# A two-layer transformer block on one core: the reciprocals of the row sums are kept in PSUM, and the bank of the weighted sums is given back behind the product that reads them

## What is computed

```
qkv = x @ w_attn + b_attn;  q, k = rope(q), rope(k)
scores = einsum('bhtd,bhsd->bhts', q, k), causal
attn = softmax(scores) * E ** (-0.5)
o = einsum('bhts,bhsd->bhtd', attn, v)        # per head: 512 rows x 32
return o @ w_proj + b_proj
```

## Time and profile before

| | us |
|---|---|
| median of 3 runs | 1322.21 |
| time of the profiled execution | 1322.04 |
| its span | 1320.3 |
| PE busy | 1192.8 (90%) |
| DVE busy | 992.8 (75%) |
| ACT busy | 766.9 (58%) |
| POOL busy | 574.8 (44%) |
| one usual iteration | 147.6 |

### The profile page before, as it was taken

The page is one execution under the profiler, slowest core; times in us unless marked ns, Lnnn a source line. Parts: engine busy times, 40 slices in busy tenths (PEclk is TensorE's granted clock), DMA queues, the critical chain, the costliest instruction groups (busy, mean ns, idle before and its releaser), DMA issues.

```text
span 1320.3 us, 24729 instructions
## 1 busy us (share of the span) xinstructions
PE 1192.8 (90%) x9300; PEld 650.0 (49%) x9300; DVE 992.8 (75%) x2884; ACT 766.9 (58%) x1410; POOL 574.8 (44%) x634
## 2 busy tenths in 40 slices
PE   6577789999999999999999999999999999988796
PEld 4123444555545554555545554555545554554352
DVE  4666976978887787968887887968887887776532
ACT  5418654666466755666466755666465755575470
POOL 1520602871159312971259313961259213961252
PEclk9786879999999999999999999999999999989799
DMA  8420221002300222012300222012300230001000
GB/s 327 126 97 2 49 69 45 1 18 68 109 1 3 57 62 76 1 24 68 104 1 2 57 80 58 1 26 66 104 1 2 57 89 16 2 9 49 9 1 32
DMA packets 47614, 65.08 MB, mean 49 GB/s; under 512 B 8549, under 2 KB 33157, under 8 KB 46087
## 3 DMA queue, kind: packets, MB, share of 16 engines
q1 hardware_dynamic: 47494, 63.51, 16.3%
HBM read 29.63 MB, written 8.39 MB: 29 GB/s over the span
## 4 chain that ended last, share of the span: by engine, by line
PE 53%; DVE 31%; ACT 9%; issue 3%; POOL 2%; DMA 1%; POOLq 0%; SPq 0%; DVEq 0%; ACTq 0%
PE gen L468 19%; PE down L511 17%; DVE score L1076 9%; PE pv L565 4%; PE score L537 4%; DVE hT L969 4%; DVE probs L969 2%; PE score L543 2%; PE gen L528 1%; DVE mx L1076 1%; POOL rstd L1402 1%; DVE qkn L1168 1%; DVE bn L1105 1%; ACT probs L817 1%; ACT qkn L761 1%
## 5 line engine op out<-in xcount | busy, mean ns | idle before, releaser
L1402 POOL TENSOR_TENSOR rstd<-veps,mhalf 128x1 f32<-128x1 f32 (+1 forms) x104 | 67.0, 645 | 503.9 <-DVE veps L1153 363.8
L817 ACT ACTIVATE probs<-score 128x512 f16<-128x512 f32 (+1 forms) x384 | 201.7, 525 | 130.5 <-PE score L537 130.4
L969 DVE TENSOR_TENSOR probs<-score,probs 128x512 f16<-128x512 f32 (+1 forms) x384 | 212.9, 595 | 64.3 <-ACT score L819 64.2
L468 PE MATMUL gen<-x2T,t1T 128*128 128x512 f16 x1024 | 242.5, 382 | 4.0 <-ACT x2T L760 2.5
L511 PE MATMUL down<-t2T,hT 128*128 128x512 f16 x1024 | 233.0, 380 | 3.5 <-DVE xn L1138 3.5
L819 ACT ACTIVATE score<-score 128x512 f32<-128x512 f32 (+1 forms) x384 | 204.5, 532 | 0.0
L468 PE MATMUL gen<-xT,wa 128*128 128x512 f16 x768 | 180.8, 387 | 4.0 <-DVE mx L1076 4.0
L1076 DVE CUSTOM_DVE_ANT_0 score<-score,mask_rows 128x512 f32<-128x512 f32 (+1 forms) x344 | 157.8, 521 | 0.0
L969 DVE TENSOR_TENSOR hT<-gen,hT 128x512 f16<-128x512 f32 x160 | 108.6, 685 | 64.0 <-ACT gen L780 25.3
L511 PEld LDWEIGHTS down<-t2T,hT 128*128 128x128 f16 x1024 | 96.5, 98 | 110.4 <-DVE xn L1138 4.7
L468 PEld LDWEIGHTS gen<-x2T,t1T 128*128 128x128 f16 x1024 | 95.4, 98 | 109.3 <-ACT x2T L760 5.2
(11 more groups left out here) (128 smaller groups left out, 1799.2 us busy)
## 6 DMA issues: line engine op xcount, KB each, us to landing
qk<-qkn SPq DMA_DIRECT2D x384, 64.0 KB, 2.0
xo<-x SPq DMA_DIRECT2D x8, 1024.0 KB, 5.6
hT<-x SPq DMA_DIRECT2D x8, 1024.0 KB, 6.5
out<-xn SPq DMA_DIRECT2D x32, 256.0 KB, 2.2
hT<-w_fc SPq DMA_DIRECT2D x4, 1024.0 KB, 13.9
hT<-w_down SPq DMA_DIRECT2D x4, 1024.0 KB, 5.4
t2T<-w_qk SPq DMA_DIRECT2D x2, 1024.0 KB, 8.5
probs<-w_v SPq DMA_DIRECT2D x1, 1024.0 KB, 18.8
```

The source lines that it names most:

```text
L468: mm = nc.tensor.matmul(bank[:, :], a, b, start=(start and n == 0), stop=(stop and n == len(pairs) - 1))
L817: nc.scalar.activation(probs[:, h % 2, HI, 512 * i:512 * i + n], score[i][:, 0:n], ACT.Exp, scale=1.0 / S_UP)
L969: return V.tensor_tensor(out, whole, hi, ALU.subtract)
```

## The change

The array `r_sum` in SBUF goes away. The reciprocals are written to columns 272 to 275 of the bank `pv`, and the product reads them there; its other input `oA` stays in SBUF. So the bank can no longer be given back by the sum L1188: that one now counts `o_sums`, for which the product waits, and the product counts `pv_drained`. The semaphore `o_ready` goes away, and what waited for it (the first turn of `xo` on PE) waits for `pv_drained`. No instruction is added, taken away or moved on any engine; an operand, an output and the semaphores change.

```
-        r_sum = sb("r_sum", [PARTS, 2, TB], f32)
...
-        H_SUM, H_SQ = 264, 268
+        H_SUM, H_SQ, R_SUM = 264, 268, 272
...
                 def o_turn(tb):
                     if tb == 0:
-                        pe.wait_ge(o_ready, HEADS * (j + 1))
+                        pe.wait_ge(pv_drained, HEADS * (j + 1))
...
                     res = pv[:, 0:VW * TB].rearrange("p (b w) -> p b w", b=TB)
-                    V.reciprocal(r_sum[:, h % 2, :], res[:, :, HD]).then_inc(o_recip, 1)
+                    V.reciprocal(pv[:, R_SUM:R_SUM + TB], res[:, :, HD]).then_inc(o_recip, 1)
                     pairs = bass.AP(pv, 0, [[512, PARTS], [VW, TB], [1, HD], [HD + 1, 2]])
-                    V.tensor_reduce(oA[:, h % 2, :, :], pairs, AX.X, ALU.add).then_inc(pv_drained, 1)
+                    V.tensor_reduce(oA[:, h % 2, :, :], pairs, AX.X, ALU.add).then_inc(o_sums, 1)
                     if h == 0 and nxt:
                         dve.wait_ge(xn_ready, TB * (j + 2))
                     dve.wait_ge(o_recip, n + 1)
-                    dve.wait_ge(pv_drained, n + 1)
+                    dve.wait_ge(o_sums, n + 1)
                     V.tensor_tensor(xo[:, :, HD * h:HD * (h + 1)], oA[:, h % 2, :, :],
-                                    r_sum[:, h % 2, :].unsqueeze(2).to_broadcast([PARTS, TB, HD]), ALU.mult
-                                    ).then_inc(o_ready, 1)
+                                    pv[:, R_SUM:R_SUM + TB].unsqueeze(2).to_broadcast([PARTS, TB, HD]), ALU.mult
+                                    ).then_inc(pv_drained, 1)
```

More of the change, by code:

```diff
@@ L278, in build @@
             sem(n) for n in ("oT_hi", "y_full", "y_ready", "xn2_ready", "x2T_hi", "fin_ready"))
-        m_neg, m_hi, o_sums, o_recip, o_ready, x1_ready = (
-            sem(n) for n in ("m_neg", "m_hi", "o_sums", "o_recip", "o_ready", "x1_ready"))
+        m_neg, m_hi, o_sums, o_recip, x1_ready = (
+            sem(n) for n in ("m_neg", "m_hi", "o_sums", "o_recip", "x1_ready"))
         bn_done = [sem(f"bn_done{i}") for i in range(4)]
```

## The result

The kernel after took 1326.93 us in the median of eight runs (1325.31 to 1328.03), the kernel before 1322.68 us (eight runs, 1320.37 to 1323.41) on the same chip: ratio 1.0035, 95% interval 1.0025 to 1.0044. The change makes the kernel slower by 0.35%, for a forecast of 0.4%. The profiled span went from 1320.3 to 1326.2 us. These 5.9 us are more than the 4.3 us between the medians: single executions of one kernel differ by 3 us, and the profiled one of the kernel after (1327.97 us) is among its longest.

A forecast was written before the change was run, and what follows sets the result against it. PE was taken to bound the usual iterations' heads 0 to 6. Terms of 7.0 (usual iterations), +0.5 (iteration 7) and -1.7 (iteration 0) gave +5.8 on 1322.04: 1327.8 us, +0.4%; 8 in 10 from 1323 to 1331.5.

The forecast's parts named there:

- The bank comes back later: Usual iterations: PE's matmul may start 0.54 us after the sum's end, not 0.15; 1.16 us each, six times 7.0 us.
- The stalls that go: DVE's products: all 20.0 us of stalls end, but 13 of them, in usual iterations, are worth nothing.
- Rival 1: Returned stalls decide, DVE being on the path in usual iterations too: 1310 us in full; chance 0.07.
- Iteration 0: DVE is the chain from head 3 to 7, so unstalled products shorten this iteration: -1.7 us.
- I take 1.8, less 0.14 for a late `weigh(14)`: Iteration 0: gain taken between 1.3 and 2.2 us, less lateness at that hand-over: -1.7 us.
- Iteration 7: Heads without queries and keys: -0.5 us at `weigh(4)` from head 1's stall, later costs; net +0.7, taken as +0.5.
- the +0.3 over heads 6 to 8: Last iteration's heads: a stall of 0.91 us gives back 0.2, two hand-overs cost 0.5.
- Price of the operands: Product with one input in PSUM stays at 0.29 us, bounds 0.28 and 0.33; nothing taken for the reciprocal.
- Rival 3: PSUM operands cost more in product and sum, +2.3 to +4.3 us on top: 1330 to 1332 us; chance 0.14.
- Rival 2: Short hand-overs' lateness is hidden, only the squares and head 14 cost: +2.0 us, 1324.0 us; chance 0.16.
- Rival 4: PE's new idle moments lower its granted clock in usual heads: 24 us more, 1352 us; chance 0.03.
- about 35: PE's waits for `pv` released by the product, not the sum: from 13 to about 35 or more in number.

The follow-up runs named there:

- run 4: The changed form in all heads but 5 and 14, which keep the form of the kernel before: 1323.50 us, ratio 1.0007 to the kernel before.
- Run 7: Kernel before with the changed form only in heads 0, 4 and 7 to 13 of every iteration: 1322.83 us, ratio 1.0003.
- run 5: Kernel before with POOL's sums of squares cut to one column in all steps but the first: 1319.20 us, ratio 0.9978.
- run 2: Kernel before with the changed form in iterations 1 to 6 alone: 1328.41 us, ratio 1.0045.
- run 6: Kernel before with the changed form only in heads 4, 5, 7 of iteration 0 and 1, 6 of iteration 7: 1318.97 us, ratio 0.9981.
- run 3: Kernel before with the changed form in iterations 0 and 7 alone: 1320.44 us, ratio 0.9991.
- run 1: Kernel before, reciprocals still in SBUF, with the bank given back behind the product in all heads: 1341.92 us, ratio 1.0148.

## Why the prediction was right, and where it was not

**The bank comes back later: right, term by term.** Starts of the weight loads in iteration 2, after against before, gave +0.11, +0.02, +0.10, +0.39, +0.13 and +0.39 us for `weigh(2)`, (3), (4), the squares, `weigh(7)` and (15); the prediction had 0.12, 0.01, 0.12, 0.39, 0.13, 0.39. That is 1.14 for 1.16, and 6.8 for 7.0 in six iterations. The 0.54 us from the sum's end to the matmul came out to a hundredth at all 15 hand-overs for which PE is listed as waiting, and run 4 takes the two large terms away alone. Run 7 shows the other side, that more than 0.54 us of distance means no cost.

**The stalls that go: right in the usual iterations.** All of them went, and in heads 1 and 2 the waits for ACT took their place; run 5 shows it for heads 0 to 2 without any late hand-over: no gain within the heads. For head 6 the kernel after shows it: behind its product, which was stalled by 0.93 us, the starts only get later, by the 0.13 us of `weigh(7)`, and stay so up to `weigh(14)`. Rival 1 (the stalls returned decide) falls there.

**Iteration 0: right place, wrong size.** The term was -1.7 and came out as -0.9. DVE's rows of the kernel after, to be read with the earlier trace rows:

```profile
145.61 0.29 DVE L1192 TENSOR_TENSOR xo<-oA,pv 128x128 f32<-128x128 f32 x1
145.81 1.67 DVE L1046 TENSOR_SCALAR hT<-hT,theta 128x2048 f32<-128x2048 f32 x1
...
149.72 2.10 DVE L1046 TENSOR_SCALAR hT<-hT,theta 128x2048 f32<-128x2048 f32 x1
```

The thresholding behind head 4 fell from 2.18 to 1.67 us, not to 1.28, and that behind head 5 only from 2.18 to 2.10: they still overlap a POOL instruction. That part of the working, by which the thresholding gets ahead of POOL's next instruction, didn't hold. Even so the lead was 1.95 us at head 8. The failed step is "I take 1.8, less 0.14 for a late `weigh(14)`": it took the lead at head 7 or 8 for what remains at the end. From head 8 to 9 it fell to 1.40, and in head 15 from 1.46 to 0.86. The window of 162 to 166 us, before and then after, in two fences (columns as in the earlier trace rows):

```profile
162.00:166.00 4.00, 1.77 (x28) 1.21 (x28) 3.62 (x15) 0.96 (x4) 2.77 (x3) 1.00 0.00 0
```
```profile
162.00:166.00 4.00, 3.24 (x25) 2.21 (x26) 2.78 (x10) 2.17 (x5) 1.92 (x2) 0.50 0.01 2
```

The kernel before had PE at 2.4 GHz (granted 1.00) there, the kernel after at 1.2 GHz (0.50). In the 4 us ahead of it PE was busy for 2.85 us before and 2.17 us after, both at the full clock still. Over all heads of this iteration the clock is 0.80, where it was 0.83:

```profile
126.00:198.00 72.00, 59.75 (x543) 35.41 (x541) 57.18 (x160) 45.13 (x96) 20.93 (x16) 0.80 0.22 57
```

That the clock took the missing 0.8 us is the likeliest reading, not shown: no run moved the clock alone, and iteration 0 with the old form differs by 0.56 us between the kernel before and run 2. In head 15 the late bank has a part: run 6, which doesn't hold it there, fell by 0.29 and not by 0.60.

**Iteration 7: +0.5 forecast, +0.5 measured, by another way.** The gain at head 1 was larger: `weigh(4)` was 0.95 us earlier than before within the iteration, not 0.5. Then the 16 down products behind it ran at half clock in part. They are shown before and after, in two fences:

```profile
1171.88 3.62 PE L511 MATMUL down<-t2T,hT 128*128 128x512 f16 x16
```
```profile
1176.94 4.68 PE L510 MATMUL down<-t2T,hT 128*128 128x512 f16 x16
```

The sum agrees by luck, and the prediction had the clock of these heads at its old level throughout. The slow stretch isn't the change's own: in run 2, with the old form there, these down products took 3.84 us, in run 3, with the new form, 3.62, and yet the heads of iteration 7 took 0.3 us less than before in run 2 and 0.3 more in run 3. The +0.39 at the squares and at head 14 stand. Of the terms between them, the +0.3 over heads 6 to 8 came out as a gain of 0.9 (in run 3 as a cost of 0.5), and the +0.15 at head 11 as nothing.

**The total: agreement in part by luck.** The profiled kernels differ by 5.9 us for a forecast of 5.8. Iteration 0 gave 0.8 us less than was taken; 0.4 us came back ahead of the first head, where nothing was changed, 0.2 in the usual iterations and 0.1 behind the heads.

**Price of the operands: right.** The product takes 288 ns where undisturbed ones took 293, so an input in PSUM costs nothing here. The two bounds were 0.28 and 0.33. The estimate of 65 ns more that followed from the Trainium skill (VectorE: DVE Perf Modes, the section on the TRN2 errata) isn't borne out; these rows decide. The reciprocal costs 9 ns more, and the sum behind it starts 0.09 us after its start as before. Rival 3 falls.

**The other rivals.** Rival 2 (short hand-overs hidden) falls: all four cost what their distances say, to a few hundredths. Rival 4 (the clock of the usual heads) falls too; the window answers to the first of the earlier trace rows:

```profile
426.00:498.00 72.00, 68.17 (x643) 39.27 (x641) 55.83 (x169) 44.79 (x97) 18.92 (x21) 1.00 0.23 64
```

DVE's busy time fell by 17.9 us, for about 20. What the prediction overstated is the count of waits: "about 35" were to be released by the product, and the trace lists 15, and 7 in front of the squares. The hand-overs that are 0.1 us late don't show as waits at all; only the shift of the start against the kernel before shows them.

## What to carry to other kernels

When a resource is to be given back one instruction later, list for each of its hand-overs the distance from the old release to the next user's start, and set it against the new minimum: only the differences below zero cost, and they add where nothing in between can absorb them. An engine's stalls are worth only what stands behind them: 20 us of stalled products gave back some 2 at most, and only where a release hung on them, as in run 1, were they dear, while a single stalled 4-element instruction cost 0.39 us an iteration. If a form helps in some heads and hurts in others, it can be chosen by head, and a small difference between the results must then be read from the iterations at full clock as well, not from the total alone.

## What the runs showed of the hardware

A DVE instruction of hardly any work can wait longest for POOL: the `tensor_scalar` over 4 elements took 0.65 us in the mean (0.81 in iteration 2), 0.17 with POOL cut short, and 0.15 over 1 element with POOL at work. The Trainium skill (SBUF — State Buffer, "Who interferes with whom") says that a DVE instruction in a 2-port mode, which a `tensor_scalar` can enter, contends with GpSimd, and that whoever issues first has the shared ports for the whole instruction while the other one blocks; with one SBUF input and outside of these modes it doesn't contend. The 0.15 and 0.81 agree with that, if one element doesn't enter the mode, which no run tells apart; the stalled one ended at 537.53 us, and the POOL instruction beside it, started at 536.24, at 537.51. Two more of this kind shrank in run 5: the last part of `m_half` from 1104 to 284 ns, its cast from 720 to 218 ns, by the groups; what they were worth wasn't told apart. And the idle moments of 0.55 us in front of the squares and 0.59 in front of `weigh(15)` left the granted clock of the usual heads at 1.00, while in iterations 0 and 7, where PE waits more, the stretches at half clock changed place with each kernel.
